# Third normalization and channel mix computed by quarters of the tokens inside the block attention's main stage

## What is computed

```python
x = x + L1_attn(layernorm(x))      # 16 heads of 8, block-causal, scores outside the block mask set to 0
x = x + L1_ffn(layernorm(x))       # channel mix

def L1_ffn(x):                     # x_prev is x one token earlier, 0 before the first token of a batch
    xr = mu_r * x + (1 - mu_r) * x_prev
    xk = mu_k * x + (1 - mu_k) * x_prev
    r = sigmoid(xr @ W_r)
    k = square(relu(xk @ W_k))
    return r * (k @ W_v)
```

## Time and profile before

| | |
|---|---|
| median of three executions | 1251.39 us (1247.80 to 1253.33) |
| the profiled execution, its own time | 1244.72 us |
| its span in the profile | 1242.9 us |
| main stage, steps 167 to 193 | 1167 to 1200.2 us |
| rest of the main stage, to the end of `add_projected` | 1200.2 to 1208.8 us |
| normalization and channel mix | 1208.8 to 1242.9 us |
| TensorE's mean granted clock | 0.931 |

### The profile page before, as it was taken

The page is one execution under the profiler, slowest core; times in us unless marked ns, Lnnn a source line. Parts: engine busy times, 40 slices in busy tenths (PEclk is TensorE's granted clock), DMA queues, the critical chain, the costliest instruction groups (busy, mean ns, idle before and its releaser), DMA issues. The chain is left out here.

```text
span 1242.9 us, 33668 instructions
## 1 busy us (share of the span) xinstructions
PE 1095.8 (88%) x13139; PEld 633.3 (51%) x13139; DVE 915.5 (74%) x1387; ACT 701.6 (56%) x1330; POOL 363.8 (29%) x239
## 2 busy tenths in 40 slices
PE   3899999999999999999999965656999999989875
PEld 2355555555455555555555555654655554554434
DVE  5988988888888889898888963336867666676326
ACT  3566666766666666766666636323155554565633
POOL 0552463355236425533552416630000000000000
PEclk8999999999999999999999976987589988898987
DMA  6866556565655566565566523112551110110001
GB/s 182 230 143 146 142 129 149 140 152 135 151 142 131 136 149 143 129 162 135 139 139 147 156 78 111 43 58 84 164 167 57 52 52 19 36 53 19 2 7 34
DMA packets 65898, 138.15 MB, mean 111 GB/s; under 512 B 13249, under 2 KB 33634, under 8 KB 61746
## 3 DMA queue, kind: packets, MB, share of 16 engines
q1 hardware_dynamic: 63842, 132.35, 42.3%
q0 software_dynamic: 1856, 4.52, 1.3%
q10 hardware_dynamic: 144, 0.52, 0.1%
HBM read 62.77 MB, written 22.41 MB: 69 GB/s over the span
## 5 line engine op out<-in xcount | busy, mean ns | idle before, releaser
L556 ACT ACTIVATE a_probs<-a_score,a_negmax 128x1024 f32<-128x1024 f32 x256 | 285.2, 1114 | 246.6 <-DVE a_negmax L641 246.6
L641 DVE TENSOR_REDUCE a_negmax<-a_score 128x1 f32<-128x1024 f32 x256 | 309.7, 1210 | 90.3 <-PE a_score L436 89.9
L1675 DVE TENSOR_REDUCE a_lowest<-a_score 128x1 f32<-128x512 f32 (+3 forms) x320 | 181.9, 631 | 78.2 <-PE a_score L1550 38.6
L1645 ACT ACTIVATE a_probs_T<-a_score_T 128x1024 f32<-128x1024 f32 (+1 forms) x192 | 146.6, 810 | 135.3 <-PE a_score_T L1530 97.3
L402 POOL TENSOR_TENSOR residual<-residual,a_scaled 128x512 f32<-128x512 f32 x62 | 79.0, 1275 | 333.5 <-ACT a_scaled L568 333.5
L647 DVE STREAM_TRANSPOSE a_probs_Tb<-a_probs 128x1024 f32<-128x1024 f32 x128 | 157.0, 1226 | 0.1
L647 DVE STREAM_TRANSPOSE a_probs_Ta<-a_probs 128x1024 f32<-128x1024 f32 x128 | 156.9, 1226 | 0.0
L436 PE MATMUL a_score<-a_k_halvesa,a_q_twicea 64*128 64x512 f32 x512 | 142.0, 642 | 12.8 <-DMA a_k_halvesa<-a_k_turned 10.9
L436 PE MATMUL a_score<-a_k_halvesb,a_q_twiceb 64*128 64x512 f32 x512 | 140.5, 635 | 1.2 <-ACT a_probs L556 1.1
L448 PE MATMUL a_acc<-a_probs_Ta,a_v_repa 32*64 32x256 f32 x4096 | 131.0, 382 | 4.0 <-ACT a_scaled L568 3.9
L448 PE MATMUL a_acc<-a_probs_Tb,a_v_repb 32*64 32x256 f32 x4096 | 126.1, 380 | 1.9 <-ACT a_scaled L568 1.9
(11 more groups left out here) (252 smaller groups left out, 1437.5 us busy)
## 6 DMA issues: line engine op xcount, KB each, us to landing
shared<-shared SPq DMA_DIRECT2D x136, 128.0 KB, 2.3
a_v_repa<-rows_v SPq DMA_DIRECT2D x64, 256.0 KB, 4.2
a_v_repb<-rows_v SPq DMA_DIRECT2D x64, 256.0 KB, 4.7
a_xn_cur<-normed_T SPq DMA_DIRECT2D x17, 512.0 KB, 3.3
rows_v<-a_v_stage SPq DMA_DIRECT2D x68, 128.0 KB, 2.4
a_q_twicea<-a_q_turned SPq DMA_DIRECT2D x32, 256.0 KB, 3.4
a_q_twiceb<-a_q_turned SPq DMA_DIRECT2D x32, 256.0 KB, 3.3
a_k_halvesa<-a_k_turned SPq DMA_DIRECT2D x32, 128.0 KB, 3.6
```

The source lines that it names most:

```text
L556: nc.scalar.activation(probs[s % 2][:], score_ps[s % 2][:], ACT.Exp, bias=negmax[:, s:s + 1], accum_out=den[:, s:s + 1]).then_inc(probs_re ...
L641: nc.vector.tensor_reduce(negmax[:, s:s + 1], score_ps[s % 2][:], axis=AX.X, op=ALU.max, negate=True)\
L1645: nc.scalar.activation(probs_T[k % 4][:, 2 * hp:2 * hp + 2, 0:hi - lo], score_T_ps[n % 2][:, :, 0:hi - lo], ACT.Exp).then_inc(pair_free, 1)
L1675: nc.vector.tensor_reduce(to, src, axis=AX.X, op=ALU.max, negate=True).then_inc(bank_free, 1)
```

## The change

`normalize` and `channel_mix` are removed, and their work becomes part of the job list of the main stage, a quarter at a time. New steps are given by tables (quarter 0, 1, 2, 3), the list is four jobs longer, and batch 1's transposes and projections come sooner:

```diff
+        WEIGHTS_AT, FRONT, TURN_X = 168, (167, 168, 187, 203), (171, 175, 190, 204)
+        KEYS, RECEPTANCE, VALUES = (174, 178, 194, 205), (174, 178, 197, 205), (177, 181, 203, 206)
+        GATES, GATED, ADDED = (195, 195, 200, 205), (199, 204, 204, 206), (199, 205, 205, 206)
-        def projected(j, after):
+        def projected(j, piece):
...
+                    if j == m * STEPS + at + ((3, 6), (2, 4))[m // G][piece]:
...
-        JOBS = range(-1, GROUPS * STEPS + 12)
+        JOBS = range(-1, GROUPS * STEPS + 16)
```

So group 7's half 0 is projected at step 185 in place of 187, and its half 1 at 200 in place of 202. In `project` the bias comes first, in one matmul of 512 columns that does not wait for `attn_T`:

```diff
-                    pe.wait_ge(bank_free, max(n - 2, bank["attn_T", m, half] + 1))
+                    pe.wait_ge(bank_free, n - 2)
+                    nc.tensor.matmul(score_ps[n % 3][:].rearrange("p (t d) -> p t d", t=4), one_row[:], bo_row[:].rearrange("o (t d) -> o t d", t=1).broadcast_to([1, 4, D]),
+                                     start=True, stop=False, skip_group_check=True)
+                    pe.wait_ge(bank_free, bank["attn_T", m, half] + 1)
                     for t in range(4):
-                        nc.tensor.matmul(score_ps[n % 3][:, t * D:t * D + D], attn_T[:, t * P:t * P + P], wo_T[:], start=True, stop=False)
-                        ins = nc.tensor.matmul(score_ps[n % 3][:, t * D:t * D + D], one_row[:], bo_row[:], start=False, stop=True)
+                        ins = nc.tensor.matmul(score_ps[n % 3][:, t * D:t * D + D], attn_T[:, t * P:t * P + P], wo_T[:], start=False, stop=True, skip_group_check=True)
```

```diff
+                def front(q):
+                    dve.wait_ge(bank_free, bank["project", q // 2 * G + G - 1, q % 2] + 1)
+                    for t in tiles:
+                        ins = nc.vector.bn_stats(out=stats[:, t, :], in_=core.x[:, t, :])
+                    step(ins)
+                    for t in tiles:
+                        ins = nc.vector.bn_aggr(out=moments[:, t, :], in_=stats[:, t, :])
+                    step(ins)
+                    step(nc.vector.tensor_scalar(var[:, cols], moments[:, cols, 1], EPS, None, ALU.add))
+                    step(nc.vector.tensor_scalar(newton[:, cols].bitcast(I32), var[:, cols].bitcast(I32), 1, None, ALU.logical_shift_right))
+                    step(nc.vector.tensor_scalar(rstd[:, cols].bitcast(I32), newton[:, cols].bitcast(I32), -1.0, 1597463007.0, ALU.mult, ALU.add))
+                    for _ in range(3):
...
+                    for t in tiles:
+                        ins = nc.vector.tensor_scalar(xn[q % 2][:, t % 4, :], core.x[:, t, :], moments[:, t, 0:1], rstd[:, t:t + 1], ALU.subtract, ALU.mult)
+                    ins.then_inc(xn_ready, 1)
+                def mix(q):
...
+                    nc.vector.tensor_scalar(xk, now, mu[:, 1:2], None, ALU.mult).then_inc(bank_free, 1)
+                    nc.vector.tensor_scalar(xr, now, mu[:, 0:1], None, ALU.mult).then_inc(r_scaled, 1)
...
+                    nc.vector.scalar_tensor_tensor(out=xk, in0=last, scalar=rest[:, 1:2], in1=xk, op0=ALU.mult, op1=ALU.add).then_inc(k_mixed, 1)
...
+                    nc.vector.scalar_tensor_tensor(out=xr, in0=last, scalar=rest[:, 0:1], in1=xr, op0=ALU.mult, op1=ALU.add).then_inc(r_mixed, 1)
+                def square(q):
...
+                    nc.vector.tensor_scalar(k_relu, score_ps[n % 3][:], 0.0, None, ALU.max).then_inc(bank_free, 1)
...
+                    nc.vector.tensor_tensor(k_sq, k_relu, k_relu, ALU.mult).then_inc(sq_done, 1)
+                def keep_receptance(q):
...
+                    nc.vector.tensor_copy(r_kept[q % 3], score_ps[n % 3][:]).then_inc(bank_free, 1)
```

`keep_value(q)` copies `v` of quarters 0 and 1 from PSUM; `gated(q)` multiplies value and gate; `added(q)` adds to the residual. Within a job VectorE's order is `front`, `gated`, `mix`, `square`, `keep_receptance`, `keep_value`, `added`. `keep_gate(q)` waits for `added(q - 2)` from quarter 2 on:

```diff
+                def keep_gate(q):
+                    act.wait_ge(bank_free, bank["r", q] + 1)
...
+                    if q >= 2:
+                        act.wait_ge(x_done, q - 1)
+                    nc.scalar.activation(gate[q % 2], r_kept[q % 3], ACT.Sigmoid).then_inc(gate_done, 1)
```

More of the change, by code:

```diff
@@ L63, in sem @@
         return self.stack.enter_context(self.nc.semaphore(name))
[L66 to L137, removed]
@@ new lines, in key, with receptance @@
+                def key(q):
+                    n = bank["k", q]
+                    pe.wait_ge(k_mixed, q + 1)
+                    pe.wait_ge(bank_free, max(n - 2, bank["weights"] + 1))
+                    nc.tensor.matmul(score_ps[n % 3][:], mix_w[:, 1, :], xk, start=True, stop=True).then_inc(bank_filled, 1)
+                def receptance(q):
+                    n = bank["r", q]
+                    pe.wait_ge(r_mixed, q + 1)
+                    pe.wait_ge(bank_free, n - 2)
+                    for t in range(4):
+                        ins = nc.tensor.matmul(score_ps[n % 3][:, t * P:t * P + P], xr[:, t * P:t * P + P], mix_w[:, 0, :], start=True, stop=True)
+                    ins.then_inc(bank_filled, 1)
@@ L1600, in project, with value @@
+                def value(q):
+                    n = bank["v", q]
+                    pe.wait_ge(sq_done, q + 1)
+                    pe.wait_ge(bank_free, n - 2)
+                    for t in range(4):
+                        ins = nc.tensor.matmul(score_ps[n % 3][:, t * P:t * P + P], k_sq[:, t * P:t * P + P], mix_w[:, 2, :], start=True, stop=True)
                     ins.then_inc(bank_filled, 1)
@@ L1622, in _ @@
                         turn(*turned(j))
[L1623 to L1626, removed]
+                    if projected(j, 0):
+                        transpose_attn(*projected(j, 0))
+                    if projected(j, 1):
+                        project(*projected(j, 1))
+                    if j == WEIGHTS_AT:
+                        turn_weights()
+                    for q in due(TURN_X, j):
+                        turn_x(q)
+                    for q in due(KEYS, j):
+                        key(q)
+                    for q in due(RECEPTANCE, j):
+                        receptance(q)
+                    for q in due(VALUES, j):
+                        value(q)
             @block.scalar
@@ L1661, in _ @@
                             keep_out((j - at) // STEPS, half)
+                    for q in due(TURN_X, j):
+                        keep_normed(q)
+                    for q in due(GATES, j):
+                        keep_gate(q)
             @block.vector
@@ L1728, in _, with added @@
+                def added(q):
+                    if q < 2:
+                        dve.wait_ge(prod_done, q + 1)
+                    else:
+                        dve.wait_ge(bank_free, bank["v", q] + 1)
+                    rows = core.x[:, 4 * q:4 * q + 4, :]
+                    nc.vector.tensor_tensor(rows, rows, gate[q % 2].rearrange("p (t d) -> p t d", t=4), ALU.add).then_inc(x_done, 1)
                 for j in JOBS:
@@ new lines, in _ @@
+                    if projected(j, 0):
+                        keep_attn_T(*projected(j, 0))
+                    if projected(j, 1):
+                        add_projected(*projected(j, 1))
+                    if j == WEIGHTS_AT:
+                        keep_weights()
+                    for q in due(FRONT, j):
+                        front(q)
+                    for q in due(GATED, j):
+                        gated(q)
+                    for q in due(TURN_X, j):
+                        mix(q)
@@ L1859, in build @@
+                    for q in due(KEYS, j):
+                        square(q)
+                    for q in due(RECEPTANCE, j):
+                        keep_receptance(q)
+                    for q in due(VALUES, j):
+                        if q < 2:
+                            keep_value(q)
+                    for q in due(ADDED, j):
+                        added(q)
 def build(nc, a, c, slots, head_rows, v_rows, out):
```

247 lines of the change are left out of this document (128 added, 119 removed).

## The result

| | before | after |
|---|---|---|
| median (executions) | 1249.60 us (4) | 1233.70 us (4) |
| ratio after / before | | 0.9866, 95% interval 0.983 to 0.9902 |
| profiled execution, own time / span | 1244.72 / 1242.9 us | 1229.90 / 1227.9 us |
| mean granted clock of TensorE, profiled execution | 0.931 | 0.939 |

The change makes the kernel 15.9 us faster by the medians. The prediction was 10.5 us, and 1233.7 us lies 1.3 us under its range.

What follows compares the result with a forecast made beforehand. TensorE was taken to bound the main stage, and a chain from engine to engine the drain and tail. -2.8 + 8.5 + 1.0 - 2.1 - 15.1 = -10.5 us gave 1240.9 us, range 1235.0 to 1248.5.

Steps and rivals of the forecast that it cites:

- Bias first: Output projections: one 512-column bias matmul ahead gains 1.4 us per projection; both in group 3 together -2.8 us.
- Main stage, +8.5 and +1.0: Interleaved steps: added matmul work and waits, less filled idle time, cost 8.5 us; a possible clock dip 1.0 more.
- The wait at step 174: First key matmul, quarter 0: TensorE waits 2.5 us for VectorE's mixed tokens.
- The wait at step 190: Turn of quarter 2's normalized rows: TensorE waits 1.2 us for VectorE's front.
- Drain -2.1: From the last value product to the last `add_projected`: 6.5 us in place of 8.6.
- tail -15.1: From the last `add_projected` to the end: one quarter of the tokens left, 19.0 us against 34.1.
- A: Interleaved steps: VectorE becomes the bound, main stage grows by 30 us, ending 11 us slower at 1262; chance 0.08.
- B: Main stage and drain: new waits drop TensorE to 1.2 GHz, +5 us, ending at 1246; chance 0.20.
- C: Tail: most links are latencies, so it keeps 25 us; total -4.5 us, 1247; chance 0.06.
- D: Main stage: idle gaps take the new work, growth only 3 us; total -16, 1235.4 us; chance 0.08.

Runs made afterwards that it cites:

- the second set: Changed kernel run again unedited, against the kernel before on the same chip: 1234.83 us, 13.3 us faster by the medians, ratio 0.9887.
- the longer fronts: Changed kernel with six Newton steps in place of three in the fronts of quarters 0 and 1, against the kernel before: 1218.92 us, ratio 0.9907.

## Why the prediction was wrong, step by step

**Bias first: the step that failed.** The prediction put it at "-2.8 us (ends 0 and -2.8)" for group 3, 1.4 more inside the main stage, and let the drain's share follow from its chain: 6.6 us in all. The runs give 9.9 (alone, with an interval of 7 to 14) and 10.0 (taken out of the changed kernel). The arithmetic part was about right. A projection takes 1.05 + 1.09 = 2.1 us in place of 3.33, a gain of 1.2 where 1.4 was said, and in the drain it is done 1.2 us after `attn_T` is kept in place of 4.3. What was missing is the clock: each old projection inside the main stage is followed by a stretch at 1.2 GHz. The rows for it lay open. The trace of before falls to 1.2 GHz at 1048.8, at 1072.7, at 1195.5 and at 1205.8, each time inside an old projection or within 2 us of its end, with 3.4, 6.8, 3.4 and (to the end of the drain) 3.0 us of lower clock. The mean clock of the timed executions rises by 0.006 with the bias first; since it has two levels, one half of the other, that is 0.006 x 2 x 1240 = 15 us less at the lower level. Were TensorE the bound in all of them, they would be worth 7.5 us; the runs leave some 3.3 us beyond the arithmetic, so the size of the clock's share is an estimate and only its sign and place are shown. I read the granted clock by stretch and not against what stood ahead of each fall, and booked the fall at 1196 as a risk of the change (+1.0) when it stands 1.3 us behind an old projection.

**How much of the miss is this step, and how much is chance.** With 10 in place of 6.6 for the bias and 3.2 in place of 3.9 for the rest the sum is 13.2 us, which is what the second set gives (13.3). The 15.9 us of the first set hold some 2.6 us more, and its profiled pair shows where such a difference can come from: the 3.3 us of the groups 2 and 5, that no part of the change touches. With the 13.3 us the time would have fallen inside the range although the step was wrong all the same, and that would have been luck.

**Main stage, +8.5 and +1.0.** Right within 1 to 1.5 us: +10.3 in the profiled pair, with 10.2 us at 1.2 GHz in it. In the second trace of the changed kernel, with no such stretch, it is 37.7 against 29.6: +8.1. The wait at step 174 was called 2.5 and was 2.1. The wait at step 190 was called 1.2 and is 1.3 in the second trace, and absent from the first, where the lower clock covers it.

**Drain -2.1 and tail -15.1.** -1.6 and -15.8. `square(2)` ahead of `divide` and `gated(0)`, `added(0)` ahead of the addition are both in the timeline. Front 4.8 (said 4.9), key 2.08 and receptance 1.91 at the lower clock (said 2.04 and 2.07), the tail 18.3 (said 19.0). The small operations on 4 columns have a pitch of 0.20, the multiply of 512 columns takes 0.48 (said 0.44), the multiply-add 0.75 (said 0.70).

**The sum without the bias.** 10.5 less 6.6 leaves 3.9 us for everything else; the changed kernel with the old projection measured 3.2 (ratio 0.9964). The structure of the forecast was right for the large part of the change and missed on the small one.

**Rivals.** A (VectorE the bound) has its place and its mechanism, and the longer fronts show VectorE on the path, but the growth is 8 to 10 us and not 30. The Trainium skill's rule (VectorE: DVE Perf Modes, the section on the TRN2 errata), a fixed cost for each small operation, agrees with the trace: 0.16 to 0.17 us for 4 columns where 16 took 0.18. It does not decide here. B (the clock pays for the new waits) is true in the changed kernel's first trace (10.2 us at 1.2 GHz from 1193), absent from the second, and seen with the longer fronts; whether the new waits brought these falls is not shown. It was outweighed by the clock that the new projection gives back. C and D fell: the tail did shrink, and the gaps did not take the work.

## What to carry to other kernels

In this kernel a matmul with one row of weights between matmuls of 128 rows cost more than its columns (0.21 us a record in place of 0.11, and granted clock behind it): lay a bias down once, in one wide matmul ahead of the others, or give it the full height. Read every fall of TensorE's clock in the trace of before against the instructions ahead of it before deciding whose cost it is, since a change that removes those instructions can get the clock back as well. And before work is woven into another stage, put VectorE's operations of one quarter in their order on paper: where one front stands between another's front and mix, the matrix engine waits.

## What the hardware showed that was not expected

- Between 128-row matmuls, a one-row matmul of 128 columns takes 0.21 us a record, and so does its neighbour; at full height both take 0.11.
- All four projections of group 3 with alternating heights were followed by 1.2 GHz, though TensorE was never idle in them (3.30 of 3.30 us busy at a clock of 1.00 in the first of them in the trace of before, 1043.65 to 1046.95); of eighteen with one wide one-row matmul ahead and two at full height none was.
- The dips that stand away from any such cause last 3.4 us each and cost a TensorE-bound group 1.65 us each (group 2: 34.9 us with none, 36.5 with one, 38.2 with two, at a clock of 1.00, 0.95 and 0.91), and their number differs between executions of one kernel. In its second set the changed kernel's fastest execution (1229.98 us) has a clock of 0.938 and its slowest (1239.31 us) 0.929.
